# The turned x1 of a four-layer kernel, made from x0 by sixteen fp32 products instead of eight turnings

## What is computed

```python
# layer 0: a dense product with W, and a low-rank one picked per sequence
H = jnp.einsum('btd,od->bto', x, W)
...
# layers 1 and 3: one 64 x 64 matrix per sequence, over the tokens
w = weights[conditions]
return jnp.einsum('bct,bcd->bdt', x, w)
...
# layer 2: causal attention, 16 heads of 32, then Wo
q = proj(hidden_states, Wq); k = proj(hidden_states, Wk); v = proj(hidden_states, Wv)
...
x = x + _L0_cond_ref(...)
x = x + _L1_cond_ref(...)
x = x + _L2_cond_ref(...)
x = x + _L3_cond_ref(...)
```

## Time and profile before

| | |
|---|---|
| median of 3 runs | 654.2 us (651.0 to 654.92) |
| profiled execution | 654.01 us, its span 652.3 us |
| TensorE's granted clock, mean of the span | 0.992 |
| PE matmuls busy | 627.8 us (96%), 7684 instructions |
| PE weight loads busy | 531.2 us (81%), 7684 |
| DVE busy | 392.0 us (60%) |
| ACT busy | 217.3 us (33%) |
| POOL busy | 140.3 us (22%) |

### The profile page before, as it was taken

One profiled execution on the slowest core, in us unless ns is written; L12 is line 12 of the kernel. 1 busy time (PEld: TensorE's weight loads), 2 busy tenths in 40 slices (PEclk: granted clock), 3 DMA queues, 4 the chain that ended last, 5 costly groups with the idle time before them and its releaser, 6 DMA issues.

```text
span 652.3 us, 19480 instructions
## 1 busy us (share of the span) xinstructions
PE 627.8 (96%) x7684; PEld 531.2 (81%) x7684; DVE 392.0 (60%) x542; ACT 217.3 (33%) x411; POOL 140.3 (22%) x113
## 2 busy tenths in 40 slices
PE   4899999999999999999999999999999999999897
PEld 3697887979888797988879798887979888797784
DVE  2567676555666655566665567656556765655363
ACT  2534342332333233233323223332232333222222
POOL 1005031140403104040310404032040402204031
PEclk8899999999999999999999999999999999999999
DMA  8440201102030110203011020301103020100101
GB/s 281 140 121 19 54 7 59 42 14 78 4 88 8 56 40 12 81 4 88 8 56 40 10 82 4 87 9 52 44 8 85 4 79 18 42 23 0 39 2 65
DMA packets 41770, 31.90 MB, mean 49 GB/s; under 512 B 16014, under 2 KB 31374, under 8 KB 41742
## 3 DMA queue, kind: packets, MB, share of 16 engines
q1 hardware_dynamic: 37790, 25.49, 14.1%
q10 hardware_dynamic: 3952, 6.03, 2.8%
HBM read 22.58 MB, written 8.91 MB: 48 GB/s over the span
## 4 chain that ended last, share of the span: by engine, by line
PE 91%; DVE 4%; issue 1%; DMA 1%; ACT 1%; ACTq 1%; POOL 0%; SPq 0%; DVEq 0%
PE banks L487 9%; PE banks L492 9%; PE banks L488 9%; PE banks L464 5%; PE banks L513 5%; PE banks L539 5%; PE banks L581 5%; PE banks L588 5%; PE banks L582 5%; PE banks L439 4%; PE banks L441 4%; PE banks L443 4%; PE banks L517 4%; PE banks L515 4%; PE banks L531 4%; PE banks L555 3%
## 5 line engine op out<-in xcount | busy, mean ns | idle before, releaser
L1122 POOL TENSOR_TENSOR probs<-probs,row_max 128x1024 f32<-128x1024 f32 x32 | 61.0, 1905 | 328.7 <-DVE row_max L966 328.7
L487 PE MATMUL banks<-x1T_hi,w_hi 128*128 128x256 f32 x512 | 130.4, 287 | 0.1
L488 PE MATMUL banks<-x1T_hi,w_lo 128*128 128x256 f32 x512 | 128.2, 283 | 0.0
L487 PEld LDWEIGHTS banks<-x1T_hi,w_hi 128*128 128x128 f32 x512 | 98.0, 191 | 1.6 <-DVE w_lo L893 0.3
L488 PEld LDWEIGHTS banks<-x1T_hi,w_lo 128*128 128x128 f32 x512 | 98.1, 192 | 0.0
L492 PE MATMUL banks<-x1T_lo,w_hi 128*128 128x256 f32 x512 | 82.3, 283 | 0.0
L492 PEld LDWEIGHTS banks<-x1T_lo,w_hi 128*128 128x128 f32 x512 | 70.6, 192 | 0.0
L952 DVE TENSOR_TENSOR qkT<-banks,beta 128x512 f32<-128x512 f32 x32 | 22.0, 691 | 58.5 <-PE banks L492 58.5
L970 DVE TENSOR_REDUCE row_sum<-probs 128x16 f32<-128x1024 f32 x32 | 39.0, 1220 | 25.7 <-ACT probs L793 25.7
L513 PE MATMUL banks<-w_hi,x1T_hi 128*128 128x512 f32 x128 | 51.6, 403 | 1.4 <-issue 0.2
L439 PE MATMUL banks<-w_hi,xT_hi 128*128 128x512 f32 x128 | 50.6, 396 | 1.0 <-DVE w_lo L893 1.0
(11 more groups left out here) (103 smaller groups left out, 1110.5 us busy)
## 6 DMA issues: line engine op xcount, KB each, us to landing
x_in<-in_x_dram SPq DMA_DIRECT2D x60, 128.0 KB, 2.7
out_dram<-x_y SPq DMA_DIRECT2D x15, 512.0 KB, 2.8
b_sel<-b_parts SPq DMA_DIRECT2D x192, 32.0 KB, 1.7
w_in<-in_L_cond_weights_dram SPq DMA_DIRECT2D x128, 16.0 KB
probsT<-in_L_cond_W_dram ACTq DMA_DIRECT2D x1, 1024.0 KB, 10.1
probs<-in_L_cond_Wk_dram ACTq DMA_DIRECT2D x1, 1024.0 KB, 8.1
qkT<-in_L_cond_Wq_dram ACTq DMA_DIRECT2D x1, 1024.0 KB, 10.2
probsT<-in_L_cond_Wv_dram ACTq DMA_DIRECT2D x1, 1024.0 KB, 6.4
```

The source lines that it names most:

```text
L487: nc.tensor.matmul(out_ap, w_hi[:, w, c, cols], x1T_hi[:, c, :], start=(c == 0), stop=False)
L488: nc.tensor.matmul(out_ap, w_lo[:, w, c, cols], x1T_hi[:, c, :], start=False, stop=False)
```

## The change

The eight turnings of `x1` are replaced by `layer1_T`: sixteen fp32 products that compute the turned layer 1 from `x0` itself. For each chunk c, tile t and sequence r the weights are the 64 rows of `x0` of that sequence and the 128 columns of that chunk, and the 64 columns of `w1_own` of that sequence pass. The results of the sequences r = 0 go to the one bank of `X1T`, those of r = 1 to the other; the copies `x1T_hi` and the rests `x1T_lo` are now by r instead of by tile, with the same sizes. `layer1` itself stays, and its copies `x1`, since the addition after `Wo` needs these rows. PE's waits for the copies move behind the attention products (the keys write layer 1's banks). Ahead of the loop the pieces come right after layer 1. ACT waits once for all sixteen instead of once for each tile; POOL builds the next `w1_own` after the pieces instead of after layer 1.

```diff
+        def x1T_of(turned_x1, r):
+            return bass.AP(tensor=turned_x1, offset=r * S, ap=[[NC * PT, P], [PT, NC], [P + (1 - 2 * r) * S, TILES], [1, S]])
+
+        def x1T_bank(r):
+            return bank[X1T[r]].rearrange("p (c t s) -> p c t s", c=NC, t=TILES)
...
-            def turn_x1(i, t, pieces):
+            def layer1_T(pieces):
                 for c in pieces:
-                    last = nc.tensor.transpose(bank[X1T[t]][:, c * P:(c + 1) * P],
-                                               x1[:, t, c * P:(c + 1) * P], ident[:])
+                    for t in range(TILES):
+                        for r in range(SEQT):
+                            last = nc.tensor.matmul(x1T_bank(r)[:, c, t, :], x0[half(r), t, c * P:(c + 1) * P],
+                                                    w1_own[half(r), t, :], start=True, stop=True)
                 if pieces[-1] == NC - 1:
                     last.then_inc(x1T_mm, 1)
...
                 pT_copied(i, 1)
-                pe.wait_ge(x1_copied_act, i + 2)
-                turn_x1(i + 1, 0, range(NC))
-                pe.wait_ge(x1_copied_dve, i + 2)
-                turn_x1(i + 1, 1, range(NC - 1))
+                layer1_T(range(NC - 1))
...
                 pT_copied(i, HG)
-                turn_x1(i + 1, 1, range(NC - 1, NC))
+                layer1_T(range(NC - 1, NC))
                 attend()
+                pe.wait_ge(x1_copied_act, i + 2)
+                pe.wait_ge(x1_copied_dve, i + 2)
                 pe.wait_ge(x1_hi_done, TILES * (i + 2))
...
             layer1()
+            layer1_T(range(NC))
             for c in (1, 2):
                 turn_part(WQ, c)
-            pe.wait_ge(x1_copied_act, 1)
-            turn_x1(0, 0, range(NC))
-            pe.wait_ge(x1_copied_dve, 1)
-            turn_x1(0, 1, range(NC))
             turn_part(WQ, 3)
             turn_part(WV, 0)
             pe.wait_ge(turned_lo, GROUPS_OF[WK][-1] + 1)
+            pe.wait_ge(x1_copied_act, 1)
+            pe.wait_ge(x1_copied_dve, 1)
             pe.wait_ge(x1_hi_done, TILES)
...
             def x1T_hi_part(i):
-                for t in range(TILES):
-                    act.wait_ge(x1T_mm, TILES * i + t + 1)
-                    copy(x1T_hi[:, :, tok(t)], in_chunks(bank[X1T[t]])).then_inc(x1_hi_done, 1)
+                act.wait_ge(x1T_mm, i + 1)
+                for q in range(SEQT):
+                    copy(x1T_of(x1T_hi, q), x1T_bank(q)).then_inc(x1_hi_done, 1)
...
             def x1T_lo_part(i):
-                for t in range(TILES):
-                    dve.wait_ge(x1_hi_done, TILES * i + t + 1)
-                    rest(x1T_lo[:, :, tok(t)], in_chunks(bank[X1T[t]]), x1T_hi[:, :, tok(t)]).then_inc(x1_split, 1)
+                for q in range(SEQT):
+                    dve.wait_ge(x1_hi_done, SEQT * i + q + 1)
+                    rest(x1T_of(x1T_lo, q), x1T_bank(q), x1T_of(x1T_hi, q)).then_inc(x1_split, 1)
...
-                    pool.wait_ge(x1_mm, TILES * SEQT * i)
+                    pool.wait_ge(x1T_mm, i)
```

## The result

The changed kernel takes 670.1 us in the median of four runs (666.6 to 673.2), the kernel before beside it 653.2 us (651.0 to 654.9): a ratio of 1.026, 95% interval 1.018 to 1.034. It is slower by 16.9 us where 13.3 were forecast; the time lies inside the range (662 to 682), at the upper end of what the main case alone had allowed (664 to 670), and 2.8 us above the forecast. The profiled execution of the changed kernel took 673.2 us, its span is 671.5 us against 652.3 before, so there are 19.2 us to account for.

What follows compares the result with a forecast made beforehand. PE was taken to bound the kernel; 15 steps x 0.76 us plus 1.94 us ahead of the loop made 13.3 us, added to the profiled 654.01 us for 667.3 us, range 662 to 682 (80%).

Steps and rivals of the forecast that it cites:

- main case: Loads of the two halves side by side, streams under loads: 667.3 us, own range 664 to 670, chance 68%.
- What bounds the kernel: PE bounds the whole kernel (91% of the chain); work leaving other engines earns nothing unless PE waits for it.
- The price of a piece: In the new products, 0.112 us for each of 16 load-stream pairs per half, with a load of about 180 ns.
- cheap load: Rival: the new pieces' loads cost as a turning's, p = 0.06 us, giving 657.1 us; chance 10%.
- Load and stream of a half: In the new pieces, streams run under the loads of the same half, 0.112 us from load to load.
- rival at 681 us: Load and stream of a half do not overlap in the new pieces: p = 0.165 us, +27 us; chance 12%.
- Halves side by side: In the new pieces, loads of the array's two row halves run beside each other, 0.112 us for each of 16.
- the rival at 695 us: The two row halves of the new pieces take turns: p = 0.22 us, +41 us; chance 8%.
- The freed wait: PE's 0.26 us stall per step for the probabilities' copies goes, within the sum; rival: a gain, faster by over 1%, 2%.
- The step and the prologue: Attention products begin 0.76 us later in each of 15 steps; the insertion ahead of the loop adds 1.94 us.
- PE idle in other places of the step would make the prediction wrong: Sign to look for in the changed profile: PE idle elsewhere in the step; no size given.

Runs made afterwards that it cites:

- The quarters: Changed kernel with thirty products on 64 x 64 weights and two left at 64 x 128: 667.7 us, ratio 1.021 to the kernel before.
- on quarters and next to layer 1: Changed kernel with only 64 x 64 pieces, second-half probabilities turned ahead of layer 1 and copied ahead of x1: 656.2 us, ratio 1.003 to the kernel before.
- with its blocks moved: 64 x 64 pieces, earlier probabilities and earlier pair 0 copies, plus 126 PE instructions at the start: 651.7 us, ratio 0.995 to the kernel before.
- moved by 94 and 126: Kernel before with 94 or 126 more PE instructions at its start: 658.4 us (ratio 1.006) and 663.0 us (1.014).

## Why the prediction was right, and where it fell short

**What bounds the kernel.** Right: the chain is PE for 90%. That work taken from DVE or ACT earns nothing was not put to a test: they have as many instructions as before (542 and 411).

**The price of a piece.** Right. 0.111 us for each load of a half against 0.112, loads of 188 ns against about 180, the two halves 7 ns apart from each other. 128 columns of a plain fp32 load lie on the line drawn through 32 and 64 columns; the turning's 140 ns is no price for other loads. So the *cheap load* (p = 0.06, 657 us) is out.

**Load and stream of a half.** That they overlap was right: 0.111 us for both, where their sum was put at 0.165 (rival at 681 us). In the run with one half after the other, 0.111 us within one half says the same. One rival was not named: a cheap load and then its stream, 0.06 + 0.055 = 0.115 us, would have nearly this pace. The quarters speak against it. In both kernels 64 columns pass; if load and stream added, and a load goes by its columns, 128 columns at 0.111 and 64 at 0.058 would leave 0.005 us for the stream. By the earlier trace rows it is at least 0.016 (layer 1's eight streams of 512 columns one after the other in 1.02 us) and at most 0.064.

The rule of the Trainium skill, "TensorE: Matmul & The Clock Gate", Part 3, by which a weight load and a matmul in flight overlap only where the row group differs, does not hold for these loads.

**Halves side by side.** Right; the rival at 695 us is out by the 7 ns, and by the 0.94 us that a step loses when the order no longer alternates.

**The freed wait.** The 0.26 us of standing are gone as forecast, and nothing more came of it.

**The step and the prologue.** 0.755 us a step against 0.76, 1.93 ahead of the loop against 1.94. The copies of ACT end 0.20 us ahead of the keys (forecast 302.62 - 302.40 = 0.22, of which 0.1 was set aside to wake PE). The one small miss is that layer 1 of pair 0 itself came 0.48 us earlier, which no step spoke of.

**What was missing from the sum.** The forecast time was 2.8 us too low, the difference of the medians 3.6, that of the profiled spans 5.9 (19.2 - 13.3). The sum took for granted that 48 more PE instructions in each step (24 loads and 24 streams) cost only their own time. They also move every later block edge, and the sum had no term for it. Three stands of 4.9 us took the place of one of 2.1, and in the profiled execution of after two of them were followed by a stretch at half clock, at 1.7 us each. "PE idle in other places of the step would make the prediction wrong" was the sentence that named it without a price, and this sign came. The time still fell into the range since the range was made wide for another reason, the rival without overlap; that it held the stands and the half clock was luck. The stand at 609.6 could be read in the trace of before, and should have been asked for: 2.12 us of "issue" in the midst of products whose operands were all there. It is no part of the change's idea, and it is as large as the whole insertion ahead of the loop.

## What to carry to other kernels

A plain fp32 load costs by its columns (0.111 us for 128, 0.058 for 64), on each tile of the array beside the others; a group of products gets that pace only if all its tiles have one shape, and two odd ones among thirty cost 0.5 us here. Making a turned result from its inputs instead of turning it paid here only where it also let the order be changed: as written it cost 2.6%, on quarters and next to layer 1 each step was 0.39 us shorter than before, and with its blocks moved the kernel was 0.5% faster. These 0.5% are no more than what the place of the blocks is worth: the kernel before, moved by 94 and 126, was 0.6% and 1.4% slower. And before a difference of one or two per cent is put down to an edit, look for stands marked "issue" at other places in both traces: instructions added on PE move the blocks in which its program arrives.

## What the runs showed of the hardware

- PE's program arrives in packets of 16 KB, 256 instructions each, and PE passes no edge of a block sooner than 1.2 us after its packet has ended (277 edges). Where the packet begins only after PE's entry into the block before, there are some 3 us from this entry to the next at the earliest; 256 instructions of small products pass in 1.5 us.
- A loop whose body of some 1018 instructions has been fetched runs on without packets (171.7 to 581.6 us in the changed kernel).
- Tiles of 64 x 64 in fp32 run four side by side with 0.058 us from load to load on each; a tile of 64 x 128 between them costs 0.36 us, a change of shape 0.1 to 0.2.
- Loads that are queued run ahead past a change of the row half: 0.055 us from load to load where two halves meet, in a program that has them one after the other.
- Semaphore increments on PE come one every 0.151 us; 64 of them at the start of its program put the first weight load off by 6.3 us (10.75 against 4.47), so they are not free as padding.
- With 126 PE instructions more in the first 9 us the changed kernel has 10.3 us at half clock from 30.4 us on, with 64 increments instead 6.8 us from the same time on, without either none there. The cause is open.
